# Attention with row maxima taken two units ahead: where the value products of a unit stand in TensorE's order

## The reference, cut to what matters

```
scores = einsum('bhid,bhjd->bhij', q, k) / sqrt(8) - slope_h * |i - j|
attn   = softmax(scores)
out    = einsum('bhij,bhjd->bhid', attn, v)
x      = layernorm(x + out @ out_w.T + out_b)
```

## Time and profile before

| | us |
|---|---|
| median of 3 runs | 705.67 (705.35 to 706.85) |
| the profiled execution: its own time | 704.49 |
| the profiled execution: its span | 702.3 |
| TensorE matmuls busy | 549.9 (78% of the span) |
| VectorE busy | 413.7 (59%) |
| ScalarE busy | 348.6 (50%) |
| reductions to the row maxima, line 510 | 297.9 in 256 |
| exponentials, line 434 | 273.3 in 512 |
| value matmuls, line 362 | 123.6 in 2048 |

### The profile page before, as it was taken

How to read it: one execution, slowest core, us unless ns; L and a number is a source line. 1 busy time by engine, 2 the same in 40 slices (tenths; PEclk the granted TensorE clock), 3 DMA queues, 4 the chain that set the end, 5 groups by cost and what they waited for, 6 DMA issues and landing times. The chain is left out here.

```text
span 702.3 us, 11576 instructions
## 1 busy us (share of the span) xinstructions
PE 549.9 (78%) x4355; PEld 291.5 (41%) x4355; DVE 413.7 (59%) x666; ACT 348.6 (50%) x660; POOL 159.1 (23%) x323
## 2 busy tenths in 40 slices
PE   4599599999999999999999999953665100999930
PEld 3324244444444444444444444323444100888820
DVE  1888367776677777777788787307685400122215
ACT  2706376676667766676667666740544000332203
POOL 4107200100100101001001010002312577245544
PEclk9858999999999999999999999985686555999985
DMA  6334711111111111111111110000000112244123
GB/s 133 109 122 118 275 30 40 35 36 37 39 40 34 42 38 31 43 34 34 43 35 35 40 41 22 7 12 0 0 0 1 35 48 63 80 132 117 51 85 116
DMA packets 46912, 39.17 MB, mean 56 GB/s; under 512 B 18118, under 2 KB 38288, under 8 KB 46859
## 3 DMA queue, kind: packets, MB, share of 16 engines
q1 hardware_dynamic: 42587, 28.49, 14.8%
q0 software_dynamic: 4272, 9.97, 4.3%
HBM read 23.42 MB, written 13.97 MB: 53 GB/s over the span
## 5 line engine op out<-in xcount | busy, mean ns | idle before, releaser
L510 DVE TENSOR_REDUCE row_max<-ps 128x1 f32<-128x1024 f32 x256 | 297.9, 1212 | 102.6 <-PE ps L330 57.9
L434 ACT ACTIVATE probs<-ps 128x512 f32<-128x512 f32 x512 | 273.3, 601 | 157.8 <-PE ps L334 95.9
L330 PE MATMUL ps<-k_stacks,q_stacks 96*128 96x512 bf16 x512 | 202.0, 400 | 15.4 <-DMA k_stacks<-qk_dram 8.0
L330 PE MATMUL ps<-q_stacks,k_stacks 99*128 99x512 bf16 x512 | 196.0, 385 | 10.6 <-DMA q_stacks<-max_dram 8.4
L362 PE MATMUL ps<-probs,v_unit 128*32 128x256 f32 x2048 | 123.6, 382 | 0.0
L334 PE MATMUL ps<-distance,slope_eye 128*128 128x128 bf16 x512 | 114.6, 224 | 0.0
L330 PEld LDWEIGHTS ps<-q_stacks,k_stacks 99*128 99x128 bf16 x512 | 50.2, 99 | 87.4 <-issue 24.0
L330 PEld LDWEIGHTS ps<-k_stacks,q_stacks 96*128 96x128 bf16 x512 | 50.2, 100 | 87.3 <-DVE row_max L510 53.8
L362 PEld LDWEIGHTS ps<-probs,v_unit 128*32 128x32 f32 x2048 | 60.1, 109 | 54.5 <-ACT probs L434 12.4
L974 ACT ACTIVATE act_t<-ps 128x640 f32<-128x640 f32 x32 | 22.5, 704 | 96.3 <-PE ps L882 96.3
L334 PEld LDWEIGHTS ps<-distance,slope_eye 128*128 128x128 bf16 x512 | 51.2, 100 | 28.6 <-issue 3.3
(11 more groups left out here) (151 smaller groups left out, 374.0 us busy)
## 6 DMA issues: line engine op xcount, KB each, us to landing
q_stacks<-qk_dram SPq DMA_DIRECT2D x96, 48.0 KB
k_stacks<-qk_dram SPq DMA_DIRECT2D x96, 48.0 KB
qk_dram<-parts SPq DMA_DIRECT2D x8, 384.0 KB, 3.6
w<-in_w SPq DMA_DIRECT2D x12, 256.0 KB, 2.9
xd<-blank POOLq DMA_DIRECT2D x8, 325.0 KB, 7.1
x_in<-xd SPq DMA_DIRECT2D x8, 325.0 KB, 4.0
yt<-zeros POOLq DMA_DIRECT2D x4, 512.0 KB, 10.0
got<-yt SPq DMA_DIRECT2D x4, 512.0 KB, 5.7
```

Source lines behind the costliest of these rows:

```text
L330: mm = pe.matmul(out, stack[slot][0:rows, blk * P:(blk + 1) * P], rhs[slot][0:rows, HALF * h:HALF * (h + 1)], start=True, stop=not on_diag ...
L434: act.activation(probs[:, k % KEPT, HALF * h:HALF * (h + 1)], ring_bank(n), ACT.Exp).then_inc(p_ready, 1)
L510: dve.tensor_reduce(row_max[:, m % 2, i:i + 1], max_pair(k).rearrange("p a n -> p (a n)"), AX.X, ALU.max).then_inc(mx_used, 1)
```

## The change

`probs` grows from 8 kept blocks to 12, and TensorE no longer makes value products behind the second group of a unit. Behind the first group of unit m it makes those of all eight blocks of unit m - 1. ScalarE's wait before it overwrites a block of `probs` follows KEPT. Nothing else is edited.

```diff
-KEPT = 2 * GROUP
+KEPT = 3 * GROUP
...
                             exp_half(m, j, h)
                             if m + 2 < UNITS:
                                 max_half(m + 2, j, h)
-                    if group == 1:
-                        values(m, 0)
-                    elif m > 0:
+                    if group == 0 and m > 0:
+                        values(m - 1, 0)
                         values(m - 1, 1)
+            values(UNITS - 1, 0)
             values(UNITS - 1, 1)
```

## The result

The changed kernel takes 723.27 us (median of 4 runs, 720.39 to 726.39) against 706.26 for the kernel before in the same comparison (705.35 to 708.1): a ratio of 1.0244, 95% interval 1.0212 to 1.0276, or 17 us slower. The forecast was 720.5, and 714 to 727. The profiled execution took 724.93 with a span of 722.8, 20.5 more than the one of before, and is itself 1.7 above the median.

The account below looks back on a forecast made before the run. SyncE's chain to the row maxima, 26.45 us per two units against TensorE's 25.08, was to bound the kernel: +13.3 to unit 28 and +1.7 at the end gave 719.5 profiled; 720.5 was taken, range 714 to 727.

Parts of the forecast that it names:

- rival A: The forecast itself: SyncE's chain to the row maxima sets each pair of units, 720.5 us; chance 0.80.
- the clock was to stay at 1.00: Sign for the profile after: TensorE's granted clock at 1.00 throughout; the forecast is wrong if it falls.
- rival C: Longer idle times halve TensorE's clock again and again, +22.5 us over 13 pairs, 743 us; chance 0.05.
- Value stretches, 3.60, and 0.23 saved at the edges: TensorE: one eight-block value stretch takes 3.60 us to the next score; one instead of two saves 0.23 a unit.
- The chain: SyncE's path from first send (9.83 us after even start) through loads to row maxima: 26.45 us per two units.
- Middle: Unit 4 starts at 115.18, then twelve pairs of 26.45 us; unit 28 starts at 432.6 against 419.32, +13.3.
- VectorE's 0.13 is lost: Eight blocks of scores between stretches, paced by VectorE's reductions, take 8.85 us against 8.72: 0.13 lost a unit.
- rival B: Faster: the chain is short enough and TensorE keeps the pace at 25.08 us a pair, 702.9 us; chance 0.07.
- Rival D, slow sends: Every send_out and round trip as long as the longest, chain 27.95 us, 19.5 more, 740 us; chance 0.08.
- Start and end: Unit 2 still starts at 87.00, first value product at 93.15; from unit 28 to last stretch 46.5 us, +1.7.
- Rival B's rule from the Trainium skill: About 2.0 us fixed plus bytes over 436 GB/s per DMA: maxima's write and read 4.0 us, not 5.7.

Follow-up runs that it names:

- e1: Kernel after the change, with the pair's eight sends issued by GpSimd instead of SyncE: 717.87 us, ratio 1.0173 to the kernel before.
- e5: As e1, but the last pair's sends issued by SyncE again: 711.98 us, ratio 1.0066 to the kernel before.
- e7: As e5, with VectorE's reciprocal in the last eight units behind the fourth reduction instead of the sixth: 705.05 us, ratio 0.9973 to the kernel before.
- e4: Kernel before the change, with ScalarE's copy two blocks later, value products unmoved: 729.33 us, ratio 1.0322 to the kernel before.
- e9: Kernel after the change, sends on SyncE, only VectorE's reciprocal moved behind the fourth reduction: 721.86 us, ratio 1.0223 to the kernel before.
- e10: Kernel after, sends on SyncE, with copy before block 4's exponentials, reciprocal behind fourth reduction, unit 1's first products early: 706.23 us, ratio 0.998 to the kernel before.
- e2: Kernel before the change, with the eight sends issued by GpSimd instead of SyncE: 713.66 us, ratio 1.0103 to the kernel before.
- e6: As e2, but the last pair's sends issued by SyncE again: 706.66 us, ratio 0.9989 to the kernel before.
- e8: As e7, with unit 1's first four blocks of value products behind unit 1's second group, as before: 704.26 us, ratio 0.9951 to the kernel before.
- e3: Kernel after the change, with ScalarE's copy ahead of block 4's exponentials instead of behind: 713.32 us, ratio 1.0101 to the kernel before.

## Why the prediction was right, and where it was off

The sign, the mechanism and the place were as forecast: rival A. The number is nearer than its terms. The sum gave 719.5 for a profiled execution, and that execution took 724.93, 5.4 more: 1.2 at the start, 2.3 in the middle, 0.8 at the end and 1.2 in the rest of the kernel, which was to stay unchanged. Within the middle, errors of both signs partly cancelled.

Of the signs named beforehand, one spoke against the forecast: the clock was to stay at 1.00, and it fell twice (rival C below). And unit 28 started without a wait, since VectorE set the pace of the units before it.

- *Value stretches, 3.60, and 0.23 saved at the edges:* 3.59 measured. TensorE's own period of 12.54 a unit was seen exactly, in e1, e5 and e7, once the chain was out of the way.
- *The chain:* first send 9.83 after the even unit's start, measured 9.82 or 9.83 in eight of the thirteen pairs; it was later in unit 2, in the two units with a fall of the clock, and in units 24 and 26, where VectorE was behind with its reciprocals. Sends had a mean of 5.23 (5.43 forecast), the round trip 3.28 (3.37), tables and parts 5.49 (5.49), the read 2.20 to 2.39 where TensorE waited for it (2.33). e4 and e1 show it from both sides: lengthened it costs, cut it costs nothing. One reading was wrong without entering the sum: the kernel before was late at three even starts (units 8, 10 and 18), not at one.
- *Middle:* from the value stretch in unit 2 to that in unit 28, 94.31 to 440.53, it was 346.2 us; 343.9 were forecast and 330.6 was before (93.15 to 423.74). The 2.3 too many have three parts. The two pairs with a fall of the clock took 28.3 and 29.8, 5.2 more than twice the forecast 26.45. The last three took 26.69, twice 13.34, which VectorE set, 0.7 more together. The other eight had a mean of 26.0, which is 3.5 less together.
- *The step that failed is "VectorE's 0.13 is lost" as a term for all units.* In the last eight units a reciprocal of 0.94 us stands among the reductions. With two short stretches a unit VectorE had enough idle time to take it; in eight blocks without a break it is on the path, 0.8 a unit. I had listed VectorE's work a unit without this one. In the kernel after moving it gave some 1.5 us (e9), less than the intervals can tell, since the chain covers most of it, but on the road to a faster kernel 6.6 (e7). Most of rival B's error is this too: it had a ratio of 702.9/705.67 = 0.996, and e5, where the maxima hold nothing up, measured 1.0066, 7.4 us more; with the reciprocal moved (e7) it was 0.9973.
- *Rival C, the clock,* had a chance of 0.05 as something in each pair. It came in 2 of 13 pairs and cost (5.94 - 4.42) + (7.17 - 4.42) = 4.3 us there. The row that I set against it had an idle time of 1.39 on the weight loads; the two falls came with 1.99 and 2.28. But the length of the idle time does not decide alone. In e9 unit 8 started after the same 1.66 us of TensorE idle (1.99 on the weight loads) and the clock held. In e4 it fell after 1.94 and twice 1.97, and held after five waits of 1.58 to 2.21. What else decides, no run here shows. First e9, then e4:

```profile
166.25 0.39 PE L330 MATMUL ps<-q_stacks,k_stacks 99*128 99x512 bf16 x1 [1.66 <-DMA q_stacks<-max_dram]
166.00:178.00 12.00, 11.59 (x108) 5.50 (x109) 7.25 (x8) 7.58 (x16) 0.98 (x5) 1.00 0.12 33
...
197.65 0.39 PE L330 MATMUL ps<-q_stacks,k_stacks 99*128 99x512 bf16 x1 [2.21 <-DMA q_stacks<-max_dram]
190.00:202.00 12.00, 9.62 (x76) 4.21 (x74) 7.77 (x7) 7.41 (x16) 0.80 (x4) 1.00 0.15 45
```

The Trainium skill (TensorE: Matmul & The Clock Gate, "HAM oscillation") describes such a loop, with a fall at every wait for a DMA of some 3 to 5 us. The trace agrees in part: only two of thirteen pairs fell, and at shorter idle times. That the kernel after spreads over 6 us between executions, with mean clocks of 0.872 to 0.879, fits with it; the falls of the other executions were not seen one by one.

- *Rival D, slow sends,* did not come: the longest `send_out` of the thirteen was 5.80.
- *Start and end:* the value stretch in unit 2 was at 94.31, not 93.15. TensorE's idle time before unit 2 was longer (8.02, not 6.75), since the first products were no longer in it, and the clock stayed at 0.50 for 10.2 us in place of 6.8. The second does not follow from the products' place: with the first products early it was 6.8 in the kernel before, e4 and e10 and 10.2 in e2, e6 and e8; with them late it was 10.2 in the kernel after, e1, e3 and e5 and 6.8 in e7 and e9. From unit 28's stretch to the last one 42.9 against 42.1, the reciprocal again.
- *Rival B's rule from the Trainium skill* (DMA: Bandwidth & Descriptors, "Anatomy of one DMA") is stated there for DMAs that GpSimd issues. It does not carry over to SyncE's queue here: 3.23 for the write and 2.36 for the read of 8 and 6 KB make 5.6 together, where the rule, an estimate, gives about 4.0.

## What to carry to other kernels

When a producer's last instructions move back, follow its consumer through every in-order queue behind it: here products on TensorE, a copy, eight sends and eight loads stood between the move and the engine that waited, and 0.35 us of slack was all there was. The cure was not to undo the move but to take the sends out of the queue that feeds the critical engine, or to let the copy go first. And before long stretches replace short ones, list everything that the other engines do in the short idle times, in each part of the run: what was free there needs a new place.

## What the runs showed of the hardware

- Sends issued by GpSimd and not SyncE cost nothing in the middle of the kernel (units of 12.64 in e2 and e6, as before), but as the last work before the hand-over to the second part they lengthened it by some 8 us (19.79 against 11.56, in e1 and e2 alike). Which part of the completion that is, no run separates.
- TensorE's clock fell to half after some idle times of 1.66 to 1.97 us (kernel after, e4, e9), for 3.4 or 6.8 us, and held after others of 1.58 to 2.21 us (e4, e9). In e1, e5 and e9 it also fell for 3.4 us in unit 31, with no idle time above 0.4 us in the 9 us before. So a single wait of this length may or may not cost a fall.
- The write of the row maxima (8 KB, to DRAM) took 2.8 to 4.0 us to its read's issue where eight loads had been issued right before it (kernel after). The 1.46 of the earlier trace rows came 2.44 behind the last load's issue; another write at that same distance took 2.90 (unit 20 of the kernel before, 323.01). And one took 2.94 with the last load 15.1 earlier (436.79). So the loads go with longer times, but they alone do not set them.
